# A rotating bank for the attention sums, and a last batch that is contracted and normalised by row tile

## What is computed

```python
q = (x @ wq).reshape(bsz, toks, NH, HD)            # 32 heads of 16
k = (x @ wk).reshape(bsz, toks, NKV, HD)           # 8 key/value heads, 4 query heads on each
v = (x @ wv).reshape(bsz, toks, NKV, HD)
scores = jnp.einsum('bqgrd,bkgd->bgrqk', qg, k) / jnp.sqrt(HD)
attn = softmax(scores, axis=-1)
x = layernorm(x + einsum('bgrqk,bkgd->bqgrd', attn, v).reshape(...) @ wo)

inter = xf @ c1_w.T @ c2_w.T                       # 1792 wide, rank 16
idx = argmax(inter in blocks of 32) + block start  # one of 32 in each of 56 blocks
h = relu(x . w1[idx])
x = layernorm(x + sum_k h[k] * w2t[idx[k]])
```

## Time and profile before

| | us |
|---|---|
| three executions | 808.32, 807.88, 806.84 |
| their median | 807.88 |
| the profiled execution: its own time | 805.32 |
| the profiled execution: span of its instructions | 803.5 |
| TensorE matmul busy in that span | 773.6 (96%) |
| VectorE busy | 656.7 (82%) |
| ScalarE busy | 394.1 (49%) |
| GpSimd busy | 337.2 (42%) |

### The profile page before, as it was taken

The page is one execution under the profiler, slowest core; times in us unless marked ns, Lnnn a source line. Parts: engine busy times, 40 slices in busy tenths (PEclk is TensorE's granted clock), DMA queues, the critical chain, the costliest instruction groups (busy, mean ns, idle before and its releaser), DMA issues.

```text
span 803.5 us, 13246 instructions
## 1 busy us (share of the span) xinstructions
PE 773.6 (96%) x4912; PEld 477.0 (59%) x4912; DVE 656.7 (82%) x839; ACT 394.1 (49%) x712; POOL 337.2 (42%) x444
## 2 busy tenths in 40 slices
PE   6999999999999999999999999999999999999994
PEld 5866433333333333333337788878878887888883
DVE  5588899999999999999226897988976897788663
ACT  5321588888888888888861331420311131002011
POOL 2212243754575456323411572544434443444441
PEclk9999999999999999999999999999999999999997
DMA  7693262344554454333406730430500030003001
GB/s 235 243 286 133 81 166 83 101 122 130 164 153 116 126 159 138 93 96 109 129 29 228 256 97 18 107 93 0 144 15 0 1 94 37 1 1 104 1 1 53
DMA packets 71816, 83.21 MB, mean 104 GB/s; under 512 B 34680, under 2 KB 38776, under 8 KB 71624
## 3 DMA queue, kind: packets, MB, share of 16 engines
q1 hardware_dynamic: 64064, 64.45, 27.1%
q0 software_dynamic: 7408, 16.81, 7.0%
q10 hardware_dynamic: 280, 1.11, 0.5%
HBM read 54.23 MB, written 28.05 MB: 102 GB/s over the span
## 4 chain that ended last, share of the span: by engine, by line
PE 87%; ACT 4%; DVE 3%; issue 3%; DMA 2%; SPq 0%; POOL 0%; ACTq 0%; POOLq 0%; DVEq 0%
PE ps_h L1312 20%; PE ps_pair L1329 19%; PE ps_pv L673 16%; PE ps_st L658 12%; PE ps_pair L641 6%; PE ps_st L616 6%; ACT stage L471 2%; PE ps_pv L616 2%; PE ps_pair L690 2%; PE ps_prep L1287 2%; ACT probs L500 2%; PE ps_prep L1282 1%; DVE neg_max L534 1%; PE ps_pair L1297 1%; PE ps_prep L1274 1%
## 5 line engine op out<-in xcount | busy, mean ns | idle before, releaser
L534 DVE TENSOR_REDUCE neg_max<-ps_pair 128x2 f32<-128x1024 f32 x256 | 310.7, 1223 | 10.9 <-PE ps_pair L641 9.2
L500 ACT ACTIVATE probs<-ps_st 128x512 f32<-128x512 f32 x493 | 268.3, 599 | 38.5 <-PE ps_st L658 20.9
L673 PE MATMUL ps_pv<-probs,v 128*32 128x256 f32 (+1 forms) x1944 | 160.8, 402 | 8.0 <-ACT stage L471 8.0
L1016 ACT ACTIVATE g_h<-picked 128x512 fp32r<-128x512 f32 x56 | 35.4, 632 | 222.7 <-DVE picked L1151 222.7
L658 PE MATMUL ps_st<-q,k 50*128 50x512 f32 x493 | 124.4, 494 | 0.2 <-ACT probs L500 0.2
L930 POOL TENSOR_TENSOR g_l<-picked,g_h 128x512 fp32r<-128x512 f32 x56 | 72.5, 1295 | 110.8 <-ACT g_h L1016 110.8
L658 PEld LDWEIGHTS ps_st<-q,k 50*128 50x128 f32 x493 | 46.5, 183 | 98.7 <-ACT probs L500 85.0
L641 PE MATMUL ps_pair<-k,q 48*128 48x512 f32 x512 | 102.1, 399 | 0.3 <-DVE neg_max L534 0.3
L673 PEld LDWEIGHTS ps_pv<-probs,v 128*32 128x32 f32 x1944 | 39.1, 107 | 97.3 <-ACT probs L500 91.8
L1312 PE MATMUL ps_h<-xt_h,w_l 128*128 128x512 f32 x224 | 89.0, 397 | 0.0
L1312 PE MATMUL ps_h<-xt_h,w_h 128*128 128x512 f32 x224 | 88.7, 396 | 0.0
(11 more groups left out here) (155 smaller groups left out, 1174.4 us busy)
## 6 DMA issues: line engine op xcount, KB each, us to landing
operands<-parts POOLq DMA_DIRECT2D x20, 512.0 KB, 3.8
q<-operands SPq DMA_DIRECT2D x64, 128.0 KB, 2.6
sums<-stage SPq DMA_DIRECT2D x32, 256.0 KB, 3.1
x_raw<-xT SPq DMA_DIRECT2D x16, 256.0 KB, 5.1
k<-operands SPq DMA_DIRECT2D x64, 64.0 KB, 2.3
q<-operands SPq DMA_DIRECT2D x64, 64.0 KB, 2.7
...
```

Of the source, the lines that this page charges most:

```text
L500: nc.scalar.activation(probs[kt % 2][:, r], score_bank(i)[:], ACT.Exp, scale=float(HD) ** -0.5).then_inc(exp_done, 1)
L534: nc.vector.tensor_reduce(neg_max[:, at:at + 2], ps_max[pair % 2][:], AX.X, ALU.max, negate=True).then_inc(max_red, 1)
L673: last = nc.tensor.matmul(ps_pv[32 * r:32 * r + VW, queries], v[b][:, kt, g], probs[kt % 2][:, r, queries], start=(kt == 0 and queries.sta ...
```

## The change

There are two parts, which share no instruction.

**Attention.** The three score banks and the bank of the sums become a ring of four. From unit 1 to unit 28 the sums of unit n go into the bank that score 3 of the unit had (`four_banks`, `sums_bank`), and from score 6 on the scores use the bank in which the previous unit's sums were. The wait for the copy of these sums (`stage_ready`) moves from the first `weigh` of unit n to score 6 of unit n (`takes_sums_bank`), where it takes the place of a wait on `exp_done`. ScalarE's order is not changed. Units 29 to 31 keep the old wait.

**The end.** In the last batch `inner_up(3, 13)` is done whole between the two halves of `inner_down(3, 11)`, and the contraction of tiles 12 and 13 goes by row tile: both m for t = 0, then for t = 1, and so on. The two parts of `picked` of the last tile go to the first columns of `xt_h0` and `xt_l0`, which are free, so `high_g` and `low_g` no longer wait on `out_mm` there. VectorE takes the variance of row tiles 0 to 2 before it adds tile 3. GpSimd takes the power for three tiles, then the shift, then the power for the fourth. ScalarE normalises tiles 0 and 1, VectorE tiles 2 and 3 by one `tensor_scalar` each. SP stores tiles 2, 0, 3; ScalarE's own queue stores tile 1.

```diff
@@ -142,12 +142,29 @@
+        def four_banks(n):
+            scores, sums_of = list(ps_st), ps_pv
+            for unit in range(1, min(n + 1, NU - AHEAD)):
+                scores[unit % 3], sums_of = sums_of, scores[unit % 3]
+            return (*scores, sums_of)
+        def takes_sums_bank(i):
+            n, at = divmod(i, TILES)
+            return at == 6 and 1 <= n < NU - AHEAD
         def score_bank(i):
+            ring = four_banks(max((i - 6) // TILES, 0))[:3]
             if i < WIDE:
-                return ps_st[i % 3]
-            return (ps_st[WIDE % 3], ps_st[(WIDE + 1) % 3], ps_max[1][:, 0], ps_max[1][:, 1], ps_st[(WIDE + 2) % 3]
+                return ring[i % 3]
+            return (ring[WIDE % 3], ring[(WIDE + 1) % 3], ps_max[1][:, 0], ps_max[1][:, 1], ring[(WIDE + 2) % 3]
                     )[(i - WIDE) % 5]
+        def sums_bank(n):
+            return four_banks(n)[3]
@@ -468,7 +485,7 @@
                     act.wait_ge(stage_out[n % 2], DMA * (n // 2))
-                nc.scalar.activation(stage[n % 2][:], ps_pv[:], ACT.Copy).then_inc(stage_ready, 1)
+                nc.scalar.activation(stage[n % 2][:], sums_bank(n)[:], ACT.Copy).then_inc(stage_ready, 1)
@@ -648,6 +665,8 @@
                     task_taken(pe, max(j for j in range(LAST) if j % 4 == i))
+                elif takes_sums_bank(i):
+                    pe.wait_ge(stage_ready, n)
                 elif i < WIDE + 2:
@@ -663,14 +682,14 @@
                 pe.wait_ge(exp_done, (step + 1) * REP)
-                if kt == 0 and n:
+                if kt == 0 and n >= NU - AHEAD:
                     pe.wait_ge(stage_ready, n)
-                elif kt == 0:
+                elif step == 0:
                     task_taken(pe, LAST - 1)
...
                 for r in range(REP):
-                    last = nc.tensor.matmul(ps_pv[32 * r:32 * r + VW, queries], v[b][:, kt, g],
+                    last = nc.tensor.matmul(sums_bank(n)[32 * r:32 * r + VW, queries], v[b][:, kt, g],
                                             probs[kt % 2][:, r, queries], start=(kt == 0 and queries.start == 0),
@@ -795,6 +814,7 @@
         out_ready, out_sent = sem("out_ready"), sem("out_sent")
+        row_ready = [sem(f"row_ready{t}") for t in range(TT)]
         block = ctx.enter_context(nc.Block())
@@ -818,6 +838,15 @@
             return own[:, W2_OWN - 1 - m] if m < W2_OWN else late[:, m - W2_OWN]
+        def picked_parts(i):
+            return (xt_h[0][:, 0], xt_l[0][:, 0]) if i == NB * MT - 1 else (g_h[i % 2][:], g_l[i % 2][:])
+        def last_rows(t):
+            row = ((NB - 1) * TT + t) * P * D
+            return out[row:row + P * D].rearrange("(p d) -> p d", p=P)
@@ -907,10 +936,9 @@
                         load_y(b)
-            for t in range(TT):
-                sp.wait_ge(out_ready, TT * (2 * NB - 1) + t + 1)
-                row = ((NB - 1) * TT + t) * P * D
-                sp.dma_start(out[row:row + P * D].rearrange("(p d) -> p d", p=P), y[0][:, t]).then_inc(out_sent, DMA)
+            for t in (2, 0, 3):
+                sp.wait_ge(row_ready[t], 1)
+                sp.dma_start(last_rows(t), y[0][:, t]).then_inc(out_sent, DMA)
             sp.wait_ge(out_sent, (NB - 1 + TT) * DMA)
@@ -925,10 +953,10 @@
                 pool.wait_ge(g_high, i + 1)
-                if i >= 2:
+                if 2 <= i < NB * MT - 1:
                     pool.wait_ge(out_mm, i - 1)
-                nc.gpsimd.tensor_tensor(g_l[m % 2][:], picked[m % 2][:], g_h[m % 2][:].bitcast(F32),
-                                        ALU.subtract).then_inc(g_ready, 1)
+                high, low = picked_parts(i)
+                nc.gpsimd.tensor_tensor(low, picked[m % 2][:], high.bitcast(F32), ALU.subtract).then_inc(g_ready, 1)
@@ -983,7 +1011,17 @@
                         root(NB + b - 1)
-            root(2 * NB - 1)
+            last, rows = 2 * NB - 1, slice(0, TT - 1)
+            pool.wait_ge(var_ready, last + 1)
+            pool.wait_ge(out_ready, TT * last)
+            nc.gpsimd.tensor_tensor(rstd[:, rows], var[:, rows], neg_half[:, rows], ALU.pow).then_inc(rstd_ready, 1)
+            pool.wait_ge(rstd_ready, last + 1)
+            nc.gpsimd.tensor_tensor(shift[:, rows], mv[:, rows, 0], rstd[:, rows], ALU.mult).then_inc(shift_ready, 1)
+            pool.wait_ge(shift_ready, 2 * last + 1)
+            nc.gpsimd.tensor_scalar(shift[:, rows], shift[:, rows], -1.0, None, ALU.mult).then_inc(shift_ready, 1)
+            pool.wait_ge(var_ready, last + 2)
+            nc.gpsimd.tensor_tensor(rstd[:, TT - 1:], var[:, TT - 1:], neg_half[:, TT - 1:], ALU.pow
+                                    ).then_inc(rstd_ready, 1)
@@ -1011,9 +1049,9 @@
                 act.wait_ge(picked_ready, i + 1)
-                if i >= 2:
+                if 2 <= i < NB * MT - 1:
                     act.wait_ge(out_mm, i - 1)
-                nc.scalar.activation(g_h[m % 2][:], picked[m % 2][:], ACT.Copy).then_inc(g_high, 1)
+                nc.scalar.activation(picked_parts(i)[0], picked[m % 2][:], ACT.Copy).then_inc(g_high, 1)
@@ -1059,7 +1097,12 @@
                         norm(NB + b - 1)
-            norm(2 * NB - 1)
+            act.wait_ge(shift_ready, 4 * NB)
+            for t in range(2):
+                nc.scalar.activation(y[0][:, t], y[0][:, t], ACT.Identity, bias=shift[:, t:t + 1],
+                                     scale=rstd[:, t:t + 1]).then_inc(row_ready[t], 1)
+            act.wait_ge(row_ready[1], 1)
+            act.dma_start(last_rows(1), y[0][:, 1]).then_inc(out_sent, DMA)
@@ -1246,13 +1289,36 @@
                         variance(NB - 1)
-            dve.wait_ge(y_in[0], DMA * (NB + 1))
-            for t in range(TT):
+            last = 2 * NB - 1
+            def last_sums(t):
                 dve.wait_ge(last_mm, t + 1)
...
                 nc.vector.bn_stats(stats[:, t], y[0][:, t]).then_inc(stat_done, 1)
-            variance(2 * NB - 1)
+            def last_variance(tiles):
+                for t in tiles:
+                    dve.wait_ge(stat_done, TT * last + t + 1)
+                    nc.vector.bn_aggr(mv[:, t], stats[:, t]).then_inc(aggr_done, 1)
+                dve.wait_ge(aggr_done, TT * last + tiles[-1] + 1)
+                at = slice(tiles[0], tiles[-1] + 1)
+                nc.vector.tensor_scalar(var[:, at], mv[:, at, 1], EPS, None, ALU.add).then_inc(var_ready, 1)
+            def last_norm(t, group):
+                dve.wait_ge(rstd_ready, last + group)
+                nc.vector.tensor_scalar(y[0][:, t], y[0][:, t], mv[:, t, 0:1], rstd[:, t:t + 1],
+                                        ALU.subtract, ALU.mult).then_inc(row_ready[t], 1)
+            dve.wait_ge(y_in[0], DMA * (NB + 1))
+            for t in range(TT - 1):
+                last_sums(t)
+            dve.wait_ge(out_ready, TT * last)
+            last_variance(range(TT - 1))
+            last_sums(TT - 1)
+            last_variance(range(TT - 1, TT))
+            last_norm(TT - 2, 1)
+            last_norm(TT - 1, 2)
@@ -1325,8 +1391,9 @@
                         pe.wait_ge(added, TT * (NB - 2) + t + 1)
-                    for n, (g, w) in enumerate(((g_h, (w2_h, wo_h)), (g_h, (w2_l, wo_l)), (g_l, (w2_h, wo_h)))):
-                        last = nc.tensor.matmul(ps_out[t][:], g[m % 2][:, t * P:(t + 1) * P], w2_tile(*w, m),
+                    high, low = picked_parts(i)
+                    for n, (g, w) in enumerate(((high, (w2_h, wo_h)), (high, (w2_l, wo_l)), (low, (w2_h, wo_h)))):
+                        last = nc.tensor.matmul(ps_out[t][:], g[:, t * P:(t + 1) * P], w2_tile(*w, m),
                                                 start=(m == 0 and n == 0), stop=(m == MT - 1 and n == 2))
@@ -1352,7 +1419,7 @@
                     i, steps = b * MT + m, slot_steps(b, m)
-                    if i == 0:
+                    if i == 0 or i == NB * MT - 1:
                         continue
@@ -1362,8 +1429,11 @@
                         step(*steps[-1])
+                    else:
+                        inner_up(NB - 1, MT - 1, (0, 1, 2, 3))
                     inner_down(*before, (2, 3))
-            inner_down(NB - 1, MT - 1, (0, 1, 2, 3))
+            for m, t in ((2, 0), (2, 1), (1, 0), (1, 1), (2, 2), (1, 2), (2, 3), (1, 3)):
+                inner_down(NB - 1, MT - m, (t,))
```

## The result

| | before | changed |
|---|---|---|
| median of 4 executions each, us | 807.45 | 797.04 |
| lowest to highest, us | 806.84 to 808.32 | 796.1 to 797.35 |
| the profiled execution, its time, us | 805.32 | 796.83 |
| its span, us | 803.5 | 795.0 |

The changed kernel is faster: the ratio is 0.9874, with a 95% interval of 0.9861 to 0.9886. In the medians that is 10.4 us, between the two profiled executions 8.5 us. What follows is worked out between profiled executions, where every us has a row.

What follows compares the result with a forecast made beforehand. TensorE, busy 96% of the span, was taken as the bound, so gains come only where it stands still or behind its last matmul. Attention 5.2 plus end 3.0, 8.2 us, takes the median from 807.88 to 799.7; range 794.4 to 803.2.

Steps and rivals of the forecast that it cites:

- the sum: Whole kernel: 5.2 us from the attention plus 3.0 from the end, 8.2 us; profiled execution 797.1, median 799.7.
- The old stall: TensorE at each change of units: the first weigh waits for ScalarE's copy of the sums, 0.37 us, 28 times.
- The new stall: TensorE at each change of units: score 7 waits for exp 4, queued behind ScalarE's copy, 0.19 us.
- The gain of the attention: Units 1 to 28: 0.18 or 0.19 us net a unit, times 28, gives 5.2 us.
- The rhythm: TensorE inside a unit: two scores_t start 1.23 us apart, the same pace as VectorE's reduces.
- The end: Behind the last matmul: earlier contraction, split norm and stores end the span 3.0 us sooner, bounds 2.2 to 3.85.
- The chain: From tile 13's pick to the stores: contraction 1.40 us earlier, epsilon 2.80 earlier, store data in one block of 2.87.
- What would show it: Profile after: 28 new scores_t waits of 0.1 to 0.2 us, units 10.0 us long, stores in one 2.9 us block.
- No new stall: Rival at the change of units: score 7 starts in time, gain 10.4 + 3.0, time 794.5 us; chance 0.12.
- The stall only moves: Rival at the change of units: the pair loses its overlap, attention gains near 1 us, time 803.9; chance 0.12.
- The ring of three becomes the bound: Rival in the attention: slower exponentials delay each of 224 score pairs, 813.1 us at 0.12 a pair; chance 0.04.
- The end gives little: Rival behind the last matmul: stores or the power take up most of the 3 us, time 801.7; chance 0.06.

Runs made afterwards that it cites:

- scores_between: Changed kernel with the scores for the unit three ahead, in the order second, first, issued between score 6 and score 7: median 792.58 us, ratio 0.9828.
- half_copy: Changed kernel with ScalarE copying only 256 of the 512 columns of the sums from unit 2 on, output not the reference's: 794.83 us.
- exp_first: Changed kernel with ScalarE taking exp 4 ahead of the copy of the sums: 807.11 us, beside 806.01 for the kernel before.
- attention_only: Kernel before with only the attention part of the change, old feed forward and end kept: median 802.04 us, ratio 0.9946.

## Why the prediction was right

**The point and the steps.** Forecast were 799.7 us, 8.2 less than before; in the profiled executions 797.1 was the sum, and 796.83 was measured. The medians fell by 10.4 and 8.2 us in two measurements. The first, 797.04, lies inside the range of 794.4 to 803.2, but 1 us below the narrower 798 to 801.5 of the sum. That the profiled execution came within 0.3 us of the sum is partly luck: the attention gave 0.9 less than forecast, the end 0.4 more, and the feed forward 0.9, for which the sum had nothing.

**The old stall, 0.37 us, 28 times.** Right where it was read: `scores_between` and `half_copy` take all stalls away and have units 0.27 to 0.35 us shorter than before. That the 8.0 us of the earlier trace rows don't show a stall in full held as well.

**The new stall, 0.19 us.** Its cause was right, exp 4 behind the copy, and two experiments that reach it from either side removed it. Its size is 0.17. Two terms of it were wrong and cancelled. I read from a duration of 0.50 that the second of a pair starts 0.11 behind the first; in the changed kernel's timeline a normal pair starts at the same instant, and both last 0.50. And I took the time from ScalarE's end to TensorE's start from the old stall, 0.15; behind exp 4 it is 0.05 (243.21 to 243.26), and in `exp_first` behind the copy 0.06. In the old stall the `weigh` behind the copy had another 0.1 before it.

**The gain of the attention, 5.2 us.** Measured 4.3 in the 28 units, 3.7 there in `attention_only` (279.86 against 283.52), and 4.4 in its median. The missing part is the rhythm. I took TensorE's 1.227 us for each half step everywhere. The first eight units of the kernel before run at 1.24, and with the change nearly all do. Where the rhythm stayed, 10.26 became 10.08, 0.18 less as forecast; where it changed, 10.18 became 10.08, which is 0.10. That is the term that was mis-sized. Another 0.9 us came in the feed forward, where I had put nothing. The wait for `xt_l` early in it comes twice in the two kernels with the old attention (1.3 and 0.9 us) and once in all ten with the new one (0.4 to 0.7), so part of it may belong to the change; why it comes less often isn't shown. The other 0.3 can't be told from chance: in the ten with the new attention the feed forward takes 369.0 to 370.5 us up to its last matmul.

**The end, 3.0 us.** Measured 3.4. The chain came as worked out: the contraction 1.38 against 1.40; from the last matmul's start to epsilon for three tiles 787.79 - 786.46 = 1.33, forecast 792.82 - 791.53 = 1.29; the first store's tile ready after 3.68, forecast 3.78. The powers of three and of one column take 0.88 and 0.81 us, where I had 1.04 for both. The normalisation on VectorE takes 0.54, between the 0.17 and the 0.69 that bounded it. By the Trainium skill (VectorE: DVE Perf Modes, Mode 2×_2P) it would run at two elements a cycle, which gives some 0.4, an estimate: 0.27 for 512 columns, and the 0.15 that a `tensor_scalar` over one column takes here. The row lies above that and below the addition's 0.69, so it doesn't settle the mode. GpSimd's power ran from 789.76 to 790.57 beside the normalisation from 789.60 to 790.14, and started 0.08 after its variance was done. The Trainium skill (SBUF — State Buffer, Who interferes with whom) has GpSimd and such an operation block each other until the first is done. The start of the power wasn't held back; whether its duration was isn't shown: four columns take 1.04, three 0.88 and one 0.81, and no row has one column without VectorE beside it. The data flowed in one block, 2.8 us long, as forecast. Of the 0.4 us that the end gave beyond the forecast, 0.14 came before the end of the data, and 0.3 behind it, in the stretch that differs by 0.3 between executions anyway.

**What would show it.** Wrong in one point: I said that the view of waits would list 28 new waits of `scores_t` for exponentials as idle time. It lists none for the matmuls, since one of two overlapping matmuls waits while the other runs. And units are mostly 10.08 us long, not 10.0.

**The rivals.** "No new stall" fell to the row at 243.26. "The stall only moves" fell too: the loss is 0.17 and not 0.37. "The ring of three becomes the bound" didn't come; exponentials still take 0.60. "The end gives little" fell: it gave 3.4.

**What stays open.** Why the matmul of `scores` takes 387 ns in some units and 396 in others, and with it a half step 1.227 or 1.24 us. Before, the switch comes at units in which VectorE also has a reciprocal, and holds until a later one; with the change it comes there too, but twice goes back within three units, where no reciprocal is. It costs 0.1 us a unit. Not the length of VectorE's reduce, as tried; nothing else was. Open as well are the 2 us between the two measurements of the medians.
